# Attention on one Trainium2 core: scores made a second time in transposed form, values in float32 on 32-column strips, instead of transposed probabilities split in two

## The reference

```python
h = _layernorm(x, axis=-1) * (1 + ca) + sa
x = x + ga * attention(h)                # then a layer norm, experts, a second layer
...
Q, K, V = split_heads(Xn @ Wq + bq), split_heads(Xn @ Wk + bk), split_heads(Xn @ Wv + bv)
scores = jnp.einsum('bhqd,bhkd->bhqk', Q, K) / jnp.sqrt(jnp.float32(D_HEAD))
scores = jnp.where(causal, scores, jnp.float32(-jnp.inf))
A = jax.nn.softmax(scores, axis=-1)
AV = jnp.einsum('bhqk,bhkd->bhqd', A, V)
return merged_heads(AV) @ Wo + bo
```

## Time and profile before

| | |
|---|---|
| timed runs, median of 3 | 1127.68 us (1126.4 to 1129.34) |
| profiled execution | span 1155.7 us from the first to the last instruction; no other time of its own is recorded |
| TensorE busy over the span | 957.4 us, 83% |
| VectorE, ScalarE, GpSimd busy | 746.7, 657.2, 458.8 us |
| granted TensorE clock, mean | 0.911 of full speed |
| from the first scores to the last sum of values | 94.9 to 343.0 us |

### The profile page before, as it was taken

How to read it: one execution, slowest core, us unless ns; L and a number is a source line. 1 busy time by engine, 2 the same in 40 slices (tenths; PEclk the granted TensorE clock), 3 DMA queues, 4 the chain that set the end, 5 groups by cost and what they waited for, 6 DMA issues and landing times. The chain is left out here.

```text
span 1155.7 us, 21305 instructions
## 1 busy us (share of the span) xinstructions
PE 957.4 (83%) x5505; PEld 801.8 (69%) x5505; DVE 746.7 (65%) x1932; ACT 657.2 (57%) x1705; POOL 458.8 (40%) x641
## 2 busy tenths in 40 slices
PE   6678799999978744687999994078989998999994
PEld 2466688888866633465899994056867777888883
DVE  4885799999974753338755552799746777444453
ACT  3568889999972333327766663367853334433331
POOL 3477556666640566501344443457620111200000
PEclk8788999999997766798999997589989998999997
DMA  7067844444404422307543434730032232102012
GB/s 250 13 210 178 216 108 91 91 91 92 91 8 138 154 75 91 133 14 253 188 129 121 130 121 151 257 116 1 12 104 70 87 108 76 47 28 65 28 56 87
DMA packets 109867, 123.53 MB, mean 107 GB/s; under 512 B 44192, under 2 KB 82848, under 8 KB 109656
## 3 DMA queue, kind: packets, MB, share of 16 engines
q1 hardware_dynamic: 101128, 99.19, 30.5%
q0 software_dynamic: 8656, 23.33, 5.5%
HBM read 77.87 MB, written 44.62 MB: 106 GB/s over the span
## 5 line engine op out<-in xcount | busy, mean ns | idle before, releaser
L746 ACT ACTIVATE PR<-PS,nmax 128x128 f32<-128x128 f32 (+3 forms) x256 | 135.6, 551 | 12.6 <-DVE nmax L786 11.2
L663 POOL TENSOR_SCALAR PR<-PR,rinv 128x128 f32<-128x128 f32 (+3 forms) x256 | 132.3, 536 | 0.0
L786 DVE TENSOR_REDUCE nmax<-PS 128x1 f32<-128x128 f32 (+3 forms) x256 | 113.7, 481 | 20.2 <-PE PS L689 14.8
L1384 POOL DMA_INDIRECT r_results<-r_y,r_to x79 | 76.0, 963 | 112.8 <-DVE r_to L1439 76.6
L794 DVE TENSOR_TENSOR PTlo<-PS,PThi 128x512 fp32r<-128x512 f32 (+1 forms) x192 | 103.1, 590 | 2.9 <-ACT PThi L756 2.9
L756 ACT ACTIVATE PThi<-PS 128x512 fp32r<-128x512 f32 (+1 forms) x192 | 96.7, 545 | 6.1 <-PE PS L701 6.0
L688 PE MATMUL PS<-K,Q 128*128 128x128 f32 (+3 forms) x256 | 83.4, 385 | 12.0 <-DMA Q<-q_parts 8.9
L701 PE MATMUL PS<-ident,PR 128*128 128x128 f32 x640 | 85.8, 279 | 3.2 <-DVE PTlo L794 2.6
L717 PE MATMUL PS<-PThi,V 128*128 128x512 f32 (+3 forms) x256 | 85.1, 345 | 1.0 <-DVE PTlo L794 0.5
L2511 DVE TENSOR_TENSOR H<-PS,H 128x256 f32<-128x256 f32 x72 | 30.6, 424 | 81.9 <-ACT H L2472 80.2
L2472 ACT ACTIVATE H<-PS 128x256 f32<-128x256 f32 x72 | 27.6, 385 | 97.2 <-PE PS L2631 96.1
(11 more groups left out here) (393 smaller groups left out, 3099.5 us busy)
## 6 DMA issues: line engine op xcount, KB each, us to landing
r_xg<-r_sorted SPq DMA_DIRECT2D x79, 129.0 KB
r_wst<-in_routed SPq DMA_DIRECT2D x16, 608.0 KB
K<-k_parts SPq DMA_DIRECT2D x64, 128.0 KB
Q<-q_parts SPq DMA_DIRECT2D x32, 128.0 KB
Q<-q_parts SPq DMA_DIRECT2D x64, 64.0 KB
V<-v_parts SPq DMA_DIRECT2D x64, 64.0 KB, 2.4
mlp_st<-r_results SPq DMA_DIRECT2D x8, 512.0 KB, 7.2
c_yg<-r_results SPq DMA_DIRECT2D x8, 512.0 KB, 8.3
```

The costliest lines, as they stand in the source:

```text
L663: pool.tensor_scalar(PR[:, e % 4, i, 0:w], PR[:, e % 4, i, 0:w], rinv[:, e % 4, i:i + 1], 1.0, ALU.mult, ALU.mult).then_inc(norm_done, 1)
L746: act.activation(PR[:, e % 4, i, 0:w], k.PS[:, i, 0:w], ACT.Exp, bias=nmax[:, e % 4, i:i + 1], accum_out=rsum[:, e % 4, i:i + 1]).then_inc ...
L786: dve.tensor_reduce(nmax[:, e % 4, i:i + 1], k.PS[:, i, 0:P * (i + 1)], AX_X, ALU.max, negate=True).then_inc(max_done, 1)
L1384: pool.indirect_dma_start(out=d.results, out_offset=bass.IndirectOffsetOnAxis(ap=to[:, i % TO_LANES:i % TO_LANES + 1], axis=0), in_=y[:, i ...
```

## The change

Heads are handled as pairs side by side, 32 *steps* of two heads:

- **Scores twice.** `scores(u)` makes a pair's scores in the old form, only for the maxima: contraction over 48 rows (high x high, low x high, high x low), head 0 on rows 0 to 47, head 1 on rows 64 to 111, into two banks; VectorE takes both heads' maxima in one instruction. The negative maximum is split in two, transposed to rows (`shift_rows`), copied by ScalarE (`shift_row`) and sent by SP into two further rows of `Q`, where `K` holds ones. `columns(u)` then makes the scores again with keys as rows and queries as columns, over 50 rows, so that the maximum is subtracted within the matmul. The mask is added by matmuls over all 128 rows in both.
- **Exponential** in three instructions a pair (both heads at once), straight into the operand of the value matmuls, in float32. The transposes of probabilities, their split, GpSimd's multiplication and the row sums are gone.
- **Values** in float32 with 32 columns a head: 16 of the value and 16 of ones (which make the sums). The four heads of a quad are written to four strips of 32 partitions of one bank. They run two steps behind the exponentials' step.
- **After the values:** the sum is copied, transposed to rows, divided by the sums, and each batch's result is transposed back in two pieces and split into `OT`, 2 x 128 rows a batch instead of 4 x 128.
- **Projections:** values go straight to SBUF in float32 (`heads.V`); their split, store and loads are gone. Keys and queries load with three row groups instead of four, eight transfers a quad instead of twelve, into one of three buffers.
- **Output product:** over two pieces instead of four, 12 matmuls a batch.

The core of the diff:

```diff
+            def scores(u):
+                def stage(x):
...
+                    if unit >= 2:
+                        pe.wait_ge(max_done, unit - 1)
+                    for j in range(2):
+                        r = slice(64 * j, 64 * j + ROWS)
+                        pe.matmul(S_BANK(u, j)[:, 0:w], Q[lane][r, p, P * i:P * i + P], K[lane][r, p, 0:w], start=True, stop=False)
+                    for j in range(2):
+                        last = pe.matmul(S_BANK(u, j)[:, w - P:w], k.identb[:], k.maskb[:], start=False, stop=True)
...
+            def columns(u):
+                def stage(x):
...
+                    wait(pe, exp_done, 3 * x + u)
+                    for n in ((0,), (1,), (2, 3))[u]:
+                        at, w = CHUNK_AT[n] - UNITS[u][0], T - P * n
+                        for j in range(2):
+                            r = slice(64 * j, 64 * j + SHIFT)
+                            pe.matmul(ST_BANK(j)[:, at:at + w], K[lane][r, p, P * n:P * n + P], Q[lane][r, p, P * n:T], start=True, stop=False)
...
+            def values(half):
...
+                    for s in range(4):
+                        last = pe.matmul(O[32 * s:32 * s + 32, P * n:T], V[:, q // QUADS, n, 4 * (q % QUADS) + s, :],
+                                         PT[:, q % 2, s, CHUNK_AT[n]:CHUNK_AT[n] + w], start=(n == 0), stop=(n == 2))
...
+            wavefront((0, scores(0)), (0, scores(1)), (2, columns(0)), (1, shift_rows), (4, values(0)), (5, quads(rows)), (6, batches(attended(0))),
+                      (0, scores(2)), (2, columns(1)), (0, scores(3)), (2, columns(2)), (4, values(1)), (6, batches(attended(1))), n=PAIRS)
...
+                    act.activation(PT[:, x // 2 % 2, 2 * (x % 2):2 * (x % 2) + 2, at:at + w], k.PS[:, 4:6, 0:w], ACT.Exp).then_inc(exp_done, 1)
...
+            for x in range(PAIRS):
+                sp.wait_ge(m_copied, x + 1)
+                for j in range(2):
+                    row = 64 * j + ROWS
+                    sp.dma_start(f32(Q[x // 2 % KQ_LANES][row:row + 2, x % 2, :]), mrow[2 * j:2 * j + 2, x % 2, :]).then_inc(m_in[x % 2], 16)
...
-                    for q in range(QUADS):
-                        last = split3(pe, k.PS[:, 4 + m, :], whi[:, q, m * P:(m + 1) * P], wlo[:, q, m * P:(m + 1) * P],
+                    for f in range(DM):
+                        last = split3(pe, k.PS[:, 4 + m, :], whi[:, f, m * P:(m + 1) * P], wlo[:, f, m * P:(m + 1) * P],
```

More of the change, by code:

```diff
@@ L61, in wait, with wavefront @@
         eng.wait_ge(sem, n)
-def wavefront(*stages):
-    for step in range(B + max(lag for lag, _ in stages)):
+def wavefront(*stages, n=B):
+    for step in range(n + max(lag for lag, _ in stages)):
         for lag, stage in stages:
-            if 0 <= step - lag < B:
+            if 0 <= step - lag < n:
                 stage(step - lag)
@@ L285, in queries @@
                 return stage
[L287 to L294, removed]
+            wavefront((0, root(0)), (4, fill), (5, root(1)), (7, queries(0)), (7, queries(1)), (7, queries(2)), (7, queries(3)), (6, store_rows))
         def scalar(act):
@@ L586, in load_keys @@
[L586 to L593 removed]
+            keys, queries = self.k.k_parts[b, q, heads], self.k.q_parts[b, q, heads]
@@ L628, in _, with batches @@
+        def batches(stage):
+            return lambda x: stage(x // (2 * QUADS)) if x % (2 * QUADS) == 2 * QUADS - 1 else None
         @block.sync
@@ new lines, in columns @@
+            def columns(u):
+                def stage(x):
+                    lane, p = x // 2 % KQ_LANES, x % 2
+                    if u == 0:
+                        pe.wait_ge(m_in[x % 2], 32 * (x // 2 + 1))
+                    wait(pe, exp_done, 3 * x + u)
[4 more added lines that the diff above has]
+                            pe.matmul(ST_BANK(j)[:, at:at + w], K[lane][r, p, P * n:P * n + P], Q[lane][r, p, P * n:T], start=True, stop=False)
+                        for j in range(2):
+                            last = pe.matmul(ST_BANK(j)[:, at:at + P], k.maskb[:], k.identb[:], start=False, stop=True)
+                    last.then_inc(st_ready, 1)
+                return stage
@@ new lines, in wait_side, with shift_rows @@
+            def wait_side(kind, i):
+                if turns:
+                    before, n = turns[-1]
+                    pe.wait_ge({"shift": m_copied, "rows": a_done, "columns": aT_lo}[before], n + 1)
+                turns.append((kind, i))
+            def shift_rows(x):
+                pe.wait_ge(shift_done, x + 1)
+                wait_side("shift", x)
+                for t in range(TT):
+                    last = pe.transpose(side(t)[0:4, :], f32(shift[:, x % 2, t].rearrange("p j a -> p (j a)")), k.ident[:])
+                last.then_inc(mT_ready, 1)
@@ new lines, in rows, with attended, stage @@
+            def rows(q):
+                pe.wait_ge(o_copied, q + 1)
+                wait_side("rows", q)
+                for t in range(TT):
+                    last = pe.transpose(side(t), osb[:, t * P:(t + 1) * P], k.ident[:])
+                last.then_inc(oT_ready, 1)
+            def attended(m):
+                def stage(b):
+                    pe.wait_ge(a_done, (b + 1) * QUADS)
+                    wait_side("columns", b * DM + m)
+                    for t in range(TT):
+                        last = pe.transpose(side(t), A[:, b % 2, t, m * P:(m + 1) * P], k.ident[:])
+                    last.then_inc(aT_ready, 1)
+                return stage
@@ new lines, in normalize @@
+            def normalize(q):
+                dve.wait_ge(oT_ready, q + 1)
+                b = q // QUADS
+                if q % QUADS == 0 and b >= 2:
+                    dve.wait_ge(aT_ready, DM * (b - 1))
+                sums = SIDE.rearrange("p (t s a d) -> p t s a d", t=TT, s=4, a=2)
+                own.link(dve.reciprocal(rinv[:], sums[:, :, :, 1, 0]))
+                own.wait()
+                cols = slice(q % QUADS * 4 * DH, (q % QUADS + 1) * 4 * DH)
+                dve.tensor_tensor(A[:, b % 2, :, cols].rearrange("p t (s d) -> p t s d", s=4), sums[:, :, :, 0, :],
+                                  rinv[:].unsqueeze(3).to_broadcast([P, TT, 4, DH]), ALU.mult).then_inc(a_done, 1)
```

381 lines of the change are left out of this document (140 added, 241 removed).

## The result

| | before | after |
|---|---|---|
| timed runs, median (lowest to highest) | 1128.51 us (1126.40 to 1130.33) | 1216.16 us (1212.37 to 1218.60) |
| profiled execution, span | 1155.7 us | 1210.7 us |
| first scores | 94.9 us | 92.8 us |
| output product starts | 346.4 us | 437.5 us |

The changed kernel is slower, by a ratio of 1.078 (95% interval 1.075 to 1.081), 88 us. The forecast was 1139 us, with a range to 1205; the time lies outside it.

A forecast was written before the change was run, and what follows sets the result against it. TensorE, or what it waits for, was taken to set each step of two heads: 7.7 us against 7.06 before. Attention's end +19 and the part behind it -8 gave +11 on the timed median, 1139 us; range 1068 to 1205.

The forecast's parts named there:

- with TensorE busy through a step I expect it to stay: Attention stage: the granted clock of 1.00, the 2.4 GHz level, was expected to stay in the changed kernel.
- One price: TensorE's step pays either row-shape changes (1.44 more) or ordered value passes (1.61 more): 7.7 us taken; chance 0.38.
- lower end of the bound: Value matmuls of a step: 1.08 us if four heads run fully side by side; 4.3 if they follow each other.
- the forecast's 3.6 and 1.44 together: TensorE's step: 3.6 us for both score passes, partly side by side, and 1.44 for changes of row shape.
- estimate of 1.8 for the values: Value matmuls of a step: 4.3 / 2.38 = 1.8 us, from a measured speedup for three column strips.
- Neither price: Attention: strips and row halves work independently, shape changes cost nothing; step 6.2 us, time 1091 us; chance 0.34.
- The wait for ScalarE: TensorE's step: the third unit of transposed scores waits 0.4 us for the second unit's exponential.
- The late row: Attention: the maximum's row arrives late, so a step can't be shorter than 5.5 to 7.8 us; about 1142 us; chance 0.04.
- The sentence on loads between two rows: SP's queue: it issues four loads between two rows of maxima; a backlog of loads would lengthen the rows' landing.
- The start: Attention's start: the first row of maxima stands behind earlier transfers on SP's queue; first transposed scores at 114 us.
- The end: Attention's end: values and last rows run about 8 us behind the last columns; end at 362 instead of 343, +19.
- Behind attention: Output product and later batches: halved matmuls and weights to split save 5 to 13 us, taken as -8.

## Why the prediction was wrong

The sum, term by term, on the way from the forecast's start of the output product (114 + 32 x 7.7 + 2, and the 3.4 us that lie behind attention's end today, 365.8) to the measured 437.5:

| term | forecast | measured | difference |
|---|---|---|---|
| first transposed scores | 114 | 115.3 | +1.3 |
| 32 steps | 32 x 7.7 | 32 x 9.58 | +60.2 |
| of it at a clock of 1.00 (7.16: run with rows on GpSimd's queue) | 32 x 7.7 | 32 x 7.16 | -17.3 |
| of it the clock | 0 | 32 x 2.42 | +77.4 |
| from the last columns to the output product | 5.4 | 15.6 | +10.2 |

This is 72 of the 77 us by which the forecast missed; the rest lies behind attention (below) or in the 4 us by which the median stands above the traced execution, 1212.4.

- **The step that failed: "with TensorE busy through a step I expect it to stay", said of the granted clock of 1.00.** I took a full PE row as what keeps the clock. It was 0.65 on a row that is 95% full, and by the table that cost 77 us. The text named a clock below 1.00 in the stage as what would make it wrong; no rival priced it. At 1.00 the forecast's mechanism holds: 7.16 for 7.7. Without those 77 us the time would have been about 1139, as forecast, but by luck: 17 us too much for the steps, and nearly as much too little for the end and what follows it.
- *One price* was the right case. Values go side by side (lower end of the bound: 1.06 for 512 columns, with the other widths about 1.4 a step against 1.08), and row shapes do cost: 7.16 with the changes, 5.80 with masks in the scores' shape, 1.36 a step, of which the masks' own streaming is a part that no run separates. The forecast had up to 1.44 for the changes alone. The Trainium skill, TensorEngine Tiling (Array Packing), Key Properties, has changes of mode drain TensorE, and these numbers agree. The scores with their masks took 4.5 in a step of 6.72, less than the forecast's 3.6 and 1.44 together. The prediction's estimate of 1.8 for the values, from the three column strips in the Trainium skill, TensorE: Matmul & The Clock Gate, Part 3, was too high: with four strips it is 1.4.
- *Neither price* could have been had by another mask: 5.80, even under the 6.2 of that rival. The scores with their masks then take 2.95 in a step, the 3.0 that the forecast had for scores wholly side by side.
- *The wait for ScalarE*, 0.36 for 0.4: right. It is 0.63 when the masks are shorter, for the exponential's own time stays.
- *The late row* did not set the changed kernel's step. The sentence on loads between two rows named the right queue but the other direction: rows did not wait behind loads, a load waited behind a row, and that set the floor of 8.5 us as soon as the step was short.
- *The start* was right to 1.3 us, by luck: SP's queue was free sooner than forecast (106.58 for 110 to 115), and the transposed scores came 8.7 us after the first row's issue, for a landing of 2.4 to 4.7. What was not seen is that the empty 11.79 us are followed by steps at a lower clock.
- *The end* was too short by 10. With no scores left, TensorE waits for single results, at a low clock (0.73 from 421.90 to 437.00):

```profile
424.13 1.94 PE L694 MATMUL PS<-PT,V 128*32 128x512 f32 x8 [0.81 <-ACT osb L724]
...
430.10 0.66 PE L704 MATMUL PS<-ident,osb 128*128 128x128 f32 x4 [0.73 <-ACT osb L724]
431.65 0.63 PE L712 MATMUL PS<-ident,A 128*128 128x128 f32 x4 [0.90 <-DVE A L778]
433.78 0.63 PE L712 MATMUL PS<-ident,A 128*128 128x128 f32 x4 [1.50 <-DVE OT L784]
437.48 0.79 PE L54 MATMUL PS<-OT,o_whi 128*128 128x512 f32 x1 [3.07 <-DVE o_wlo L1034]
```

- *Behind attention*, the -8 can't be checked closely. Batch 0's 12 products took 5.3 us (437.48 to 442.77) for 8.4. What reached the end is 1 us by the traces without before's 35 us, 3 by the medians (88 for 91) and 7 by the time of the traced execution itself (84 for 91).

What stays open is what exactly lowers the clock on a full row. Steps of the same matmuls ran at 1.00 and at 0.50 in one execution, so the mix of matmuls alone does not decide. Adding full-array matmuls brought the clock to 1.00 for 25 steps with every change of shape still there; taking the changes of row shape between scores and masks away, with no full-array work added, brought it to 0.90 over the stage. Half-filled arrays, the emptying between shapes, or both may do it; no run was made that parts them.

## What to carry to other kernels

A busy row of TensorE does not tell the clock it runs at: read the granted clock of the stage beside it, and when a change turns full-array matmuls into partial ones with gaps or changes of shape, price the stage at both levels. Keep neighbouring matmuls in one row shape, masks included. When a step gets shorter, look at each queue for a load that stands behind something made late in the step before: it becomes the new bound, and here the clock was lower behind that wait too.

## What the runs showed of the hardware that was not expected

- TensorE was granted 1.2 GHz over 17 us in which its row was busy for 16.94. The Trainium skill, TensorE: Matmul & The Clock Gate, Part 1, has the clock follow how busy the engine is; the busy row is not that measure here.
- Matmuls of zeros that nothing needs made a kernel faster: 25 us for 256 of them in the changed kernel with rows on GpSimd's queue, 11 us by the medians for 64 placed inside a wait (5 of them seen in attention by the traces).
- Two heads' score matmuls run side by side on the two row halves, but for the widest chunk the gain shows only if the masks share its row shape: two heads' chunk with its masks took 0.66 us with masks over all rows and 0.41 with masks in the scores' shape; one head's took 0.30 before.
- Four heads' float32 values on four column strips take 1.06 us for eight passes of 512 columns.
